# Four cross-attention layers on one core: smaller mask and key row work, tokens turned in other places, and own order lists for the first round and the end

## The reference

```python
# wide (layers 0 and 2)
q = hidden_states @ Wq;  k = ctx @ Wk;  v = ctx @ Wv
col_bias[:, token_indices_A] = (-20.0 * (1.0 - mask_A))[:, None]
col_bias[:, token_indices_B] = (-20.0 * (1.0 - mask_B))[:, None]
probs = softmax(q @ k.T * 64 ** -0.5 + col_bias)
out = (probs @ v) @ Wo + bo + residual
...
# narrow (layers 1 and 3)
xn = rmsnorm(x, norm_w);  q = xn @ wq;  k = cond @ wk;  v = cond @ wv
out = residual + (softmax(q @ k.T * 0.25) @ v) @ wo
```

## Time and profile before

| | us |
|---|---|
| median of 3 runs | 1842.65 (1836.5 to 1844.34) |
| the profiled execution | 1840.65 |
| its span in the trace | 1838.9 |
| TensorE busy (matmul) | 1658.9 |
| VectorE busy | 1226.8 |
| ScalarE busy | 1023.5 |
| GpSimd busy | 462.2 |

### The profile page before, as it was taken

How to read it: one execution, slowest core, us unless ns; L and a number is a source line. 1 busy time by engine, 2 the same in 40 slices (tenths; PEclk the granted TensorE clock), 3 DMA queues, 4 the chain that set the end, 5 groups by cost and what they waited for, 6 DMA issues and landing times. The chain is left out here.

```text
span 1838.9 us, 29698 instructions
## 1 busy us (share of the span) xinstructions
PE 1658.9 (90%) x10732; PEld 898.9 (49%) x10732; DVE 1226.8 (67%) x2370; ACT 1023.5 (56%) x1729; POOL 462.2 (25%) x327
## 2 busy tenths in 40 slices
PE   5898587999999999999999998999999999998553
PEld 5787443444544554444544454545454545453322
DVE  4438564666868776778776866777877787776332
ACT  2111054676766676667666765676667666765131
POOL 4233302122322231223132322131313131312201
PEclk9889698999999999999999999999999999999786
DMA  8976362041215121513253225221513151212105
GB/s 271 317 259 231 115 151 49 24 92 37 75 36 120 30 76 34 117 32 77 68 121 89 67 44 109 52 80 33 106 43 78 35 105 44 78 35 63 29 20 200
DMA packets 177816, 167.39 MB, mean 91 GB/s; under 512 B 91649, under 2 KB 132989, under 8 KB 176136
## 3 DMA queue, kind: packets, MB, share of 16 engines
q1 hardware_dynamic: 175368, 155.01, 32.9%
q10 hardware_dynamic: 2304, 10.49, 1.4%
HBM read 118.78 MB, written 46.63 MB: 90 GB/s over the span
## 5 line engine op out<-in xcount | busy, mean ns | idle before, releaser
L1195 DVE TENSOR_REDUCE tops<-general 128x2 bf16<-128x308 f32 x1024 | 434.3, 472 | 107.7 <-PE general L1290 50.4
L1054 ACT ACTIVATE probs<-score_ps 128x512 f32<-128x512 f32 x512 | 299.3, 598 | 175.4 <-PE score_ps L1330 160.5
L1151 POOL TENSOR_TENSOR kept<-kept,inv_b 128x512 f32<-128x512 f32 x128 | 167.0, 1326 | 427.3 <-DMA inv_b<-scratch_inverses 427.3
L1182 DVE CAST q_aux<-q_pair 64x512 bf16<-64x512 f32 x160 | 81.3, 508 | 191.5 <-ACT q_pair L1042 190.6
L1064 ACT ACTIVATE q_aux<-general 4x512 bf16<-4x512 bf16 x320 | 187.5, 586 | 29.2 <-PE general L1301 23.6
L1041 ACT ACTIVATE q_pair<-general 64x512 fp32r<-64x512 f32 x160 | 94.6, 591 | 157.1 <-PE general L1275 156.0
L1139 POOL TENSOR_TENSOR x_lo<-xn,x_hi 128x1024 fp32r<-128x1024 f32 x32 | 75.8, 2369 | 328.2 <-ACT x_hi L1022 184.4
L1290 PE MATMUL general<-w_top,q_aux 128*128 128x154 bf16 x1024 | 130.9, 234 | 27.7 <-DVE q_pair L1185 16.9
L1228 DVE TENSOR_TENSOR x<-general,x 128x512 f32<-128x512 f32 x160 | 106.8, 689 | 69.3 <-PE general L1389 68.2
L1090 ACT ACTIVATE a_hi<-kept 128x512 fp32r<-128x512 f32 x160 | 93.6, 624 | 103.1 <-PE general L1389 41.3
L1208 DVE TENSOR_TENSOR a_lo<-kept,a_hi 128x512 fp32r<-128x512 f32 x160 | 121.7, 793 | 39.4 <-ACT a_hi L1090 38.8
(11 more groups left out here) (150 smaller groups left out, 3262.1 us busy)
## 6 DMA issues: line engine op xcount, KB each, us to landing
inv_b<-scratch_inverses SPq DMA_DIRECT2D x128, 256.0 KB, 4.8
xn<-scratch_stream SPq DMA_DIRECT2D x16, 512.0 KB, 3.4
w_pair<-scratch_wk_hi SPq DMA_DIRECT2D x32, 256.0 KB
x<-scratch_stream SPq DMA_DIRECT2D x16, 512.0 KB, 3.5
inv_n<-scratch_inverses SPq DMA_DIRECT2D x256, 32.0 KB, 1.8
scratch_stream<-x SPq DMA_DIRECT2D x16, 512.0 KB, 4.6
scratch_wk_hi<-p_kout_hi SPq DMA_DIRECT2D x16, 308.0 KB
p_raw<-in_L_xattn_Wk_dram SPq DMA_DIRECT2D x4, 1024.0 KB, 7.2
```

What stands on the lines that cost most here:

```text
L1054: nc.scalar.activation(dst, score_ps[:, number % 2, :], ACT.Exp, scale=scale).then_inc(act_exp.sem, 1)
L1151: last = nc.gpsimd.tensor_tensor(tiles[i], tiles[i], (inv_b, inv_n)[n % 2][:, i, :], ALU.mult)
L1195: last = nc.vector.tensor_reduce(tops[:, n % 2, sub, 2 * pair:2 * pair + 2], src, AX_X, ALU.max)
```

## The change

It has four parts.

*Rows.* The mask tiles have 16 partitions of 128 elements in place of one of 2048, and are worked behind pieces 5 to 8. The key rows of both pairs are made together in five operations behind piece 10, with a broadcast comparison. They are stored by eight DMAs at piece 12.

*Tokens.* The eight groups are turned ahead of pieces 0, 1, 3, 5, 7, 9, 11 and 13.

*First round.* `FIRST` is a list that replaces the start of the plan up to step 9 of window 1 (478 entries). It has the same entries in another order.

*End.* `LAST` replaces the plan from step 11 of window 6 on, with the same entries in another order and two new ones. `fetch` loads a finished group of `stream` into the space of `wq[0]`, and `give` turns half a group on TensorE (four token blocks' transposes, 2 x 2), copies it by ScalarE into the space of `w_val` or `inv_b`, and SyncE stores the 256 KB to `out`. Groups 6 and 7 are given from `x` itself. `store_outputs` calls `layers`, and its former body is gone, with the two last stores of `x` to `stream`.

```diff
-                if i < NX:
-                    take_stream(i)
+        STREAM = (0, 1, 3, 5, 7, 9, 11, 13)
+                if i in STREAM:
+                    take_stream(STREAM.index(i))
...
-        mrow = sb("p_mrow", [1, 2, S])
+        mrow = sb("p_mrow", [16, P])
...
-                for j in range(4):
-                    link(nc.vector.tensor_scalar(onehot[:, j, :], keynof[:], idxf[:, 2, 4 * p + j:4 * p + j + 1], None, ALU.is_equal))
-                link(nc.vector.tensor_tensor(onehot[:, 0, :], onehot[:, 0, :], onehot[:, 1, :], ALU.max))
-                link(nc.vector.tensor_tensor(onehot[:, 2, :], onehot[:, 2, :], onehot[:, 3, :], ALU.max))
-                link(nc.vector.tensor_scalar(onehot[:, 4, :], onehot[:, 2, :], -1.0, 1.0, ALU.mult, ALU.add))
-                link(nc.vector.tensor_tensor(onehot[:, 1, :], onehot[:, 0, :], onehot[:, 4, :], ALU.mult))
-                for r in range(6):
-                    link(nc.vector.tensor_copy(keyrow[:, p, r, :], onehot[:, 1 if r < 3 else 2, :]))
+                every = [1, 8, KEYS]
+                link(nc.vector.tensor_tensor(onehot[:], keynof[:, None, :].to_broadcast(every),
+                                             idxf[:, 2, :, None].to_broadcast(every), ALU.is_equal))
+                pairs = onehot[:].rearrange("o (s two) k -> o s two k", two=2)
+                link(nc.vector.tensor_tensor(chosen[:], pairs[:, :, 0], pairs[:, :, 1], ALU.max))
+                sides = chosen[:].rearrange("o (p s) k -> o p s k", s=2)
+                link(nc.vector.tensor_scalar(free[:], sides[:, :, 1], -1.0, 1.0, ALU.mult, ALU.add))
+                link(nc.vector.tensor_tensor(keyrow[:, :, 0], sides[:, :, 0], free[:], ALU.mult))
+                link(nc.vector.tensor_copy(keyrow[:, :, 1], sides[:, :, 1]))
...
-                if i == 10:
+                if i == 5:
                     make_mask_values()
-                elif 11 <= i < 14:
-                    make_mask_part(i - 11)
-                elif i == 14:
+                elif 6 <= i < 9:
+                    make_mask_part(i - 6)
+                elif i == 9:
                     make_key_numbers()
-                elif 15 <= i < 17:
-                    make_key_rows(i - 15)
+                elif i == 10:
+                    make_key_rows()
...
+FIRST = """
+    wkeys 0 0, early 0, split 0, wkeys 0 3, query 0 0, query 0 1, query 1 0, max 0 0, max 0 1, max 0 2,
...
+LAST = """
...
+                    elif what == "fetch":
+                        i = FETCHES.index(c)
+                        if i < 2:
+                            wait(sp, pe_query.sem, pe_query.after(ITER - 1, "query", 11, 1))
+                        else:
+                            wait(sp, pe_give.sem, max(pe_give.after(ITER - 1, "give", FETCHES[i - 2], part) for part in range(2)))
+                        sp.dma_start(fetch_to[:, i % 2], dr["stream"][c // 2, c % 2]).then_inc(fetched[i % 2], 16)
+                    elif what == "give":
+                        wait(sp, act_give.sem, act_give.after(w, what, c, k))
+                        slot = GIVES.index((c, k)) % 4
+                        to = out.rearrange("b (c t p) d -> (b c) p t d", t=4, p=P)[c][:, 2 * k:2 * k + 2, :]
+                        sp.dma_start(to, give_to[slot].rearrange("p (t d) -> p t d", t=2)).then_inc(given[slot], 16)
...
+                    for t in range(2):
+                        for c in range(KC):
+                            at = (2 * k + t) * P
+                            last = nc.tensor.transpose(ps[:, t * C + c * P:t * C + c * P + P], of[:, c, at:at + P], ident[:])
```

More of the change, by code:

```diff
@@ L629, in plan @@
         entries += [(r + turn, what, n, k) for what, n, k, turn in WINDOW if present(r + turn, what, n)]
-    return entries
+    first = [(turn, what, n, k) for what, n, k, turn in window(FIRST)]
+    assert sorted(first) == sorted(entries[:len(first)])
+    entries[:len(first)] = first
+    last = [(ITER - 1 + turn, what, n, k) for what, n, k, turn in window(LAST)]
+    known = [x for x in last if x[1] not in ("fetch", "give")]
+    assert sorted(known) == sorted(entries[len(entries) - len(known):])
+    return entries[:len(entries) - len(known)] + last
 PLAN = plan()
+FETCHES = [n for w, what, n, k in PLAN if what == "fetch"]
+GIVES = [(n, k) for w, what, n, k in PLAN if what == "give"]
 class Signal:
@@ L655, in wait, with layers @@
         eng.wait_ge(sem, value)
-GENERAL = [(*x, m) for x in PLAN if x[1] in ("query", "max", "turn", "output", "square", "rate")
+GENERAL = [(*x, m) for x in PLAN if x[1] in ("query", "max", "turn", "output", "square", "rate", "give")
            for m in range(KC if x[1] == "output" else 1)]
 USE = {use: i for i, use in enumerate(GENERAL)}
-def run_layers(nc, ins, dr):
+def layers(nc, ins, dr, out):
     ctx = ExitStack()
@@ L748, in run_layers, with made_by @@
         pool_scale, dve_low = signal("pool_scale", "scale"), signal("dve_low", "low")
+        pe_give, act_give = signal("pe_give", "give"), signal("act_give", "give")
+        fetched, given = [sem(f"fetched{i}") for i in range(2)], [sem(f"given{i}") for i in range(4)]
         reader = {"query": dve_query, "max": dve_max, "turn": act_turn, "output": dve_output,
-                  "square": dve_square, "rate": dve_rate}
+                  "square": dve_square, "rate": dve_rate, "give": act_give}
+        fetch_to = wq[0][:].bitcast(F32).rearrange("p a (k n) -> p a k n", n=TOK)
+        give_to = [w_val[:, 0:TOK], w_val[:, TOK:2 * TOK], inv_b[:, 0, :], inv_b[:, 1, :]]
+        def made_by(o):
+            return (B + o // 2 + o % 2, "output", 1 if o % 2 else 3, 1)
         block = ctx.enter_context(nc.Block())
@@ L1012, in _ @@
             each_entry()
+            for slot in range(4):
+                sp.wait_ge(given[slot], 16 * B)
         @block.scalar
@@ L1082, in do @@
                         nc.scalar.activation(wide_sums[:], sum_ps[:], ACT.Copy).then_inc(act_sums.sem, 1)
+                elif what == "give":
+                    wait(act, pe_give.sem, pe_give.after(it, what, n, k))
+                    i = GIVES.index((n, k))
+                    if i < 2:
+                        wait(act, pe_value.sem, pe_value.after(ITER - 1, "value", 11, 1))
+                    elif i < 4:
+                        wait(act, pool_scale.sem, pool_scale.after(ITER - 1, "scale", 2, 3))
+                    else:
+                        act.wait_ge(given[i % 4], 16 * (i // 4))
+                    nc.scalar.activation(give_to[i % 4], bank_of((it, what, n, k, 0)), ACT.Copy).then_inc(act_give.sem, 1)
                 elif what == "norm":
@@ L1390, in do @@
                         last.then_inc(pe_output.sem, 1)
+                elif what == "give":
+                    if n < 6:
+                        i = FETCHES.index(n)
+                        pe.wait_ge(fetched[i % 2], 16 * (i // 2 + 1))
+                    else:
+                        wait(pe, dve_output.sem, dve_output.after(*made_by(n)))
+                    ps = bank((it, what, n, k, 0))
+                    of = fetch_to[:, i % 2] if n < 6 else x[:, n % 2]
+                    for t in range(2):
+                        for c in range(KC):
+                            at = (2 * k + t) * P
+                            last = nc.tensor.transpose(ps[:, t * C + c * P:t * C + c * P + P], of[:, c, at:at + P], ident[:])
+                    last.then_inc(pe_give.sem, 1)
                 elif what == "square":
@@ L1410, in _, with run_layers @@
             each_batch(pe, do)
+def run_layers(nc, ins, dr):
+    dr["ins"] = ins
 def store_outputs(nc, dr, out):
[L1415 to L1472 removed]
@@ L1476 @@
+    layers(nc, dr["ins"], dr, out)
 _INS = ["x", "ctx_2048", "mask_S_fk1", "mask_S_fk0"]
```

238 lines of the change are left out of this document (164 added, 74 removed).

## The result

The changed kernel takes 1795.43 us (median of 4 runs, 1792.7 to 1801.82) against 1840.24 us for the kernel before (4 runs). The ratio is 0.9761, with a 95% interval of 0.9725 to 0.9797. The forecast was 1790.3 with a range of 1770 to 1811, so direction and size came out. Of the terms behind it the first round's was far off, and others made up for part of it.

What follows compares the result with a forecast made beforehand. TensorE was taken to bound the kernel, with idle or low-clock time in preparation, first round and tail. Gains 7.0 + 11.6 + 1.5 - 1.5 + 4.5 + 7 + 22.3 = 52.4 us from 1842.65 gave 1790.3, range 1770 to 1811.

Steps and rivals of the forecast that it cites:

- Items 1 and 3: Preparation: mask and key rows over more partitions gain 7.0 us; their stores moved to piece 12 gain 1.5 us.
- first-use price: Preparation, VectorE: a first mask operation costs 3.9 us extra, a first key-row operation up to 4.0 us.
- Item 2: Preparation: tokens over more pieces remove TensorE stops of 3.2 and 6.4 us and low clock behind them; gain 11.6 us.
- Item 4: First round's list: earlier queries and split gain 3 and 14.5, ScalarE's stand and late outputs cost 15 and 4; -1.5 us.
- rival B: First round: the stand is dear, item 4 at -12 us with chunk 0's outputs late; 1801 us, chance 0.15.
- Item 5: Tail's list: sums ahead of maxima gain 4.5 us; the order behind the last query start gains 7 us.
- Item 6: Closing part: most token groups stored before the end, 6.6 us instead of 28.9 behind the last add; gain 22.3 us.
- Rival E: Tail: waits in SP's single queue before output stores and fetches delay the scaling chains; slower, 1864 us, chance 0.03.
- The clock rule: Preparation, 97 to 120 us: the low clock stays though TensorE is busy; nothing counted, against 5.1 us by the skill's rule.
- the end of the preparation near 193: Sign of being right: the preparation ends at about 193 us instead of 213.
- The squares of the tail: Sign of being right: squares stand 11.9 us before the last query, with score matmuls between.
- No stop over 3 us: Sign of being right: in the preparation TensorE has no stop over 3 us.

Runs made afterwards that it cites:

- stream8: Changed kernel with the eight groups of tokens turned ahead of pieces 0 to 7 again, new rows kept: 1800.43 us, ratio 0.977 to the kernel before.
- early_load: Changed kernel with SyncE's load of chunk 2's tokens issued ahead of the narrow chunks' initial loads: 1779.58 us, ratio 0.9638 to the kernel before.
- control: The changed kernel itself, run again with no edit as measure for other experiments: 1792.22 us, ratio 0.9733 to the kernel before.
- early_outs: early_load with six buffers for the products of the preparation in place of four: 1770.28 us, ratio 0.9628 to the kernel before.

## Why the prediction held, point by point

**Items 1 and 3, the rows.** 7.0 + 1.5 were predicted, and 15.0 are measured alone, 9.8 on top of the tokens. The stops were right, and 3.3 of the 15.0 stood before the rows could act (see above), so 11.7 are to be explained. Two steps were wrong. First, 2.3 were taken off because a first-use price would make VectorE block for 4.3 us behind piece 5 and hold the narrow value products. In the changed kernel those two mask operations took 0.89 and 0.22, in stream8 0.20 and 1.27, and TensorE has no stop on `p_nvout` in either. The "first use" does not exist: it was GpSimd. Second, the lower clock behind the stops was counted for the tokens in item 2, but not here. The earlier trace rows give the stops, and these stretches what lay behind them: two of the kernel before, then two of stream8, which has the new rows only.

```profile
150.00:165.00 15.00, 12.79 (x64) 10.07 (x65) 13.98 (x32) 0.42 (x1) 4.45 (x2) 0.89 0.70 243
179.00:197.00 18.00, 11.73 (x49) 10.54 (x49) 12.51 (x39) 0.00 (x0) 4.51 (x2) 0.53 0.19 62
```

```profile
170.00:180.00 10.00, 8.97 (x47) 8.44 (x47) 2.14 (x11) 1.89 (x2) 5.74 (x2) 0.65 0.65 233
180.00:195.00 15.00, 14.39 (x56) 10.99 (x54) 3.34 (x5) 0.00 (x0) 0.00 (x0) 0.89 0.20 73
```

Only the time in which TensorE worked counts, since a stop is in the sum already. Busy 12.79 us at 0.89 and 11.73 at 0.53 lack 1.4 and 5.5. In stream8, 8.97 at 0.65 and 14.39 at 0.89 lack 3.1 and 1.6. So the clock behind the row stops was worth about 2 us, an estimate from these rows. Item 3 was smaller than said: TensorE stood 13.40 us in front of the first query before and 12.50 in stream8, 0.9 in place of 1.5.

**Item 2, the tokens.** 11.6 predicted, 11.5 alone, 6.3 on top of the rows. "What is late next" was named as DMA and given a fifth, 2.9. What came was DMA at another place, the landing of product stores: 5.2 less for both edits together than for each alone, with 6.5 us of stops on `p_vout` against 1.0 and 1.4 with one edit. How much of the 5.2 is that and how much the difference of single traces is open (see the table of first queries).

**Item 4, the first round.** This is the term that was mis-sized: -1.5 predicted, -11.2 and -9.8 measured, the size of rival B. The mechanism was right: a stand of about 12 us behind the turn of step 2, released by the load (14.68), from about 272 to 284 in old time, which is 252 to 264 in new (TensorE stood from 248.5 to 262.68); sums at 307 less 20, so 287 (284.25). The stand's cost, put at 15 + 4, is 14.6, so it was not too low. What failed is the gain set against it: 3 + 14.5 for the early queries and for the stop of 5.20 with the clock behind it. The list without the stand brings 6.2 over the old one, in place of 17.5; and the old list itself lost 2.8 behind the shorter preparation. So -2.8 + 6.2 - 14.6 = -11.2. I had counted the small stops and the low clock behind the old stop as if the new order had none. It has some: in early_load, from 271 to 284, TensorE waits 1.9, 1.7 and 1.1 us for turned maxima and query parts.

**Item 5, the list of the end.** 4.5 + 7 predicted. In the changed kernel's profile the squares (1717.39 against 1721.42 in the earlier trace rows) lost 2.0 on the lead at step 11 of round 6. In control they gained 2.2. The first scores behind the last query gained another 8.7 and 8.6, and the four last steps 2.0 and 2.3. So the second term was right or a little low, and of the first at most half came. The prediction had the copy of the sums 2.8 us sooner and the reciprocal 4.5. Beyond the lead that stood at step 11, the copy came 2.3 us later in the changed kernel's profile (1666.86) and 0.5 sooner in control (1655.90), the reciprocal 0.3 and 3.0 sooner (1671.25 and 1660.35). From the copy to the reciprocal it takes 4.4 us in both, where 7.0 had been, so the wait behind VectorE's maxima did shrink; it is the copy that did not move up. The scalings behind the reciprocal then followed at 8.2, 9.6 and 8.8 us (8.3, 8.8 and 8.8 in control), where 8.9, 8.3 and 8.1 had been. The waits there are on broadcasts in a queue that now also carries fetches; whether these cost it, no run separates.

**Item 6, the closing part.** 22.3 predicted, 24.2 and 23.4 measured. The landing was taken as 2.6 and is 2.4, as against the 7.3 that the full queue had. Rival E, the waits in SyncE's queue, did not come at its size: the only long new wait of TensorE on a fetch was covered, and no two scalings of one chunk stand 10 us apart.

**The clock rule.** What the row of 97 to 120 showed came again. Stretches of early_outs, in which TensorE has no stop before or in the narrow value products (us, then busy us by engine, granted clock, DMA share, GB/s):

```profile
80.00:85.00 5.00, 5.00 (x27) 5.00 (x27) 0.87 (x6) 0.00 (x0) 2.99 (x2) 0.50 1.04 391
85.00:90.00 5.00, 5.00 (x21) 4.44 (x21) 3.09 (x7) 1.91 (x1) 1.61 (x1) 0.56 0.80 243
90.00:95.00 5.00, 5.00 (x23) 4.03 (x22) 4.66 (x4) 1.92 (x1) 3.76 (x2) 1.00 0.94 314
```

TensorE is busy 5.00 of 5.00 us, and the clock is 0.50 (1.2 GHz) and 0.56 of full, then 1.00 again. A TensorE without gaps did not stay fast. The narrow value products start every 0.11 us from 76.13 on and last 0.28 each by the profile, so their records overlap; how full the array was behind them no run shows, and the cause of the fall stays open. By the rule of the Trainium skill (TensorE: Matmul & The Clock Gate, Part 1), that activity releases the throttle, the prediction's sum would have been 5.1 us higher. If activity is what the profile calls busy, the trace does not agree with it for this stretch, and the sum rightly left it out.

Together: without the first round 53.9 us were predicted. The changed kernel's profile gained 50.1 and control's 60.6, and the stretch with the same list makes up 5 of that difference. The first round then took 11.2 and 9.8 of it, where 1.5 was set. That miss of 8 to 10 us is the one that matters; preparation and closing part gave 1 to 3 us more each than their terms, and the medians ended 5 us (the changed kernel) and 2 us (control) above the forecast. That the preparation's 21.3 came so near to the 20.1 of the forecast is in part luck: the rows' 8.5 is 6.5 below what was measured alone, and 5.2 went the other way where the two edits met.

Of the signs named in advance, these came: the end of the preparation near 193 (the first load behind the barrier leaves at 191.65), the stand of ScalarE released by the load, the last store within 3 us of the last add. The squares of the tail stand 10.0 us ahead of the last query (1717.39 and 1727.35), not 11.9, with score matmuls between. "No stop over 3 us" failed by the 3.6 above. The long comparison did take 5.32 us, and behind it TensorE stood 0.9 (at 136.30).

## What to carry to other kernels

When an instruction is moved ahead on one engine, look up the DMA that it needs in the queue that issues it. Here one `dma_start` in the wrong place of SyncE's queue turned a gain of 6 us into a loss of 8, and moving it made the kernel about 1% faster (ratios of 0.9638 and 0.9658 against 0.9761 and 0.9733). When two edits each remove stops, don't add their gains: what both uncover (here four product buffers) takes its share once, and the next buffer is worth a look. Price each removed stop with the lower clock behind it, in every item or in none, and only for the time in which TensorE works. And before a VectorE operation that is far too long is called a first use, look whether it ends with a GpSimd one.

## What the runs showed of the hardware that was not expected

Casts, `TENSOR_SCALAR` operations and `TENSOR_TENSOR` operations of VectorE that work from SBUF to SBUF were held for the whole rest of a GpSimd operation that had begun before them: 0.20 us became 3.69, 0.23 became 4.60, and 1.43 became 5.32, each ending with or shortly behind GpSimd's end. The first mask operation of the changed kernel is one too (0.89 us where stream8 has 0.20). Operations of VectorE that read PSUM were not, nor was the reciprocal of 128x64, which took 0.54 us inside a GpSimd subtraction (at 455.43) as outside. Order of time, VectorE, changed kernel: the same cast outside of any subtraction, and inside the one from 134.31 to 138.89.

```profile
118.16 0.69 DVE L279 CAST p_kout_hi<-p_ps 128x512 fp32r<-128x512 f32 x1 [0.49 <-PE p_ps L447]
...
136.07 0.68 DVE L279 CAST p_kout_hi<-p_ps 128x512 fp32r<-128x512 f32 x1
```

The Trainium skill (SBUF — State Buffer, Who interferes with whom) says that the port pair which the two engines share is locked for a whole instruction; the traces agree, with the numbers above. In the preparation it costs TensorE little, since it may run three products ahead. It goes on in the attention part: of the 160 casts `q_aux<-q_pair` of L1377 in the changed kernel, the 33 that begin inside a GpSimd operation of more than 0.9 us take 1.13 us in the middle, the others 0.42; of the 160 `a_lo` subtractions, 25 take 1.50 and the others 0.68. What that costs there, no run shows.

The load of `xn` landed 3.4 us behind its issue at 256.64, and 11.3 us behind its issue at 220.28, in a stretch full of other loads. That is still 14 us ahead of the split that reads it (245.43).
